# A graph network's gathers start ahead of the last chunk's table, with that chunk's share added from counts, and strip work moved into the layer's end

## What is computed

```python
h = relu(layernorm(x)); h = relu(h @ enc_w1.T + enc_b1) @ enc_w2.T + enc_b2
for w in conv_w:                                   # 5 layers
    m = h @ w
    agg = segment_sum(m[src], dst, num_segments=12500)
    gi, gh = agg @ gru_wih.T + gru_bih, h @ gru_whh.T + gru_bhh
    r, z = sigmoid(ir + hr), sigmoid(iz + hz)      # thirds of gi and gh
    n = tanh(i_n + r * h_n)
    h = (1 - z) * n + z * h
h = relu(h)
x + sigmoid(relu(h @ dec_w1.T + dec_b1) @ dec_w2.T + dec_b2)
```

## Time and profile before

| | |
|---|---|
| timed runs, median (lowest, highest) | 4899.29 us (4897.4, 4904.11) |
| profiled execution, span from the first to the last instruction | 4906.3 us |
| PE busy | 4601.4 us, 94% |
| ACT busy | 3823.5 us, 78% |
| POOL busy | 3459.9 us, 71% |
| DVE busy | 2117.3 us, 43% |
| DMA | 1215.98 MB, mean 248 GB/s |

### The profile page before, as it was taken

The page is one execution under the profiler, slowest core; times in us unless marked ns, Lnnn a source line. Parts: engine busy times, 40 slices in busy tenths (PEclk is TensorE's granted clock), DMA queues, the critical chain, the costliest instruction groups (busy, mean ns, idle before and its releaser), DMA issues.

```text
span 4906.3 us, 65249 instructions
## 1 busy us (share of the span) xinstructions
PE 4601.4 (94%) x21744; PEld 3523.0 (72%) x21744; DVE 2117.3 (43%) x5021; ACT 3823.5 (78%) x3047; POOL 3459.9 (71%) x3554
## 2 busy tenths in 40 slices
PE   5579999999799999989999999899999989999998
PEld 3357767776587777767777777677777767777775
DVE  7678878878423333332333333232323322333334
ACT  5479999998588888858888887788878758787785
POOL 3577667666477777767777777677777767767675
PEclk8789999999999999999999999999999989999999
DMA  6899999999877777787777779777777877777775
GB/s 210 282 287 278 282 279 289 271 279 293 280 231 240 241 234 245 233 297 243 234 239 241 236 241 310 225 239 235 247 229 248 289 235 225 221 214 220 217 219 154
DMA packets 711002, 1215.98 MB, mean 248 GB/s; under 512 B 282849, under 2 KB 441570, under 8 KB 710562
## 3 DMA queue, kind: packets, MB, share of 16 engines
q1 hardware_dynamic: 540992, 748.04, 49.5%
q0 software_dynamic: 169264, 462.12, 29.9%
q10 hardware_dynamic: 434, 1.81, 0.1%
HBM read 1015.23 MB, written 196.41 MB: 247 GB/s over the span
## 4 chain that ended last, share of the span: by engine, by line
PE 69%; ACT 9%; POOL 7%; issue 6%; DMA 5%; DVE 3%; SPq 1%; DVEq 0%; POOLq 0%; ACTq 0%
PE strip_ps L1908 33%; PE four_ps L1908 16%; POOL messages L940 7%; ACT counts L1126 6%; PE agg_ps L1801 3%; PE four_ps L1801 3%; DMA raw<-adjacency 3%; ACT room L1101 2%; PE r_ps L1817 2%; PE z_ps L1817 1%; PE r_ps L1823 1%; PE z_ps L1823 1%; PE four_ps L1824 1%; PE r_ps L1830 1%; PE four_ps L1894 1%
## 5 line engine op out<-in xcount | busy, mean ns | idle before, releaser
L940 POOL DMA_INDIRECT messages<-table,src_stage x3503 | 3412.8, 974 | 1355.4 <-issue 1088.3
L1126 ACT ACTIVATE counts<-raw 128x2048 fp32r<-128x2048 uint8 x1382 | 2277.8, 1694 | 408.7 <-PE strip_ps L1908 222.7
L1908 PE MATMUL strip_ps<-counts,parts 128*128 128x512 f32 x9212 | 2338.7, 407 | 65.6 <-ACT counts L1126 55.3
L1908 PEld LDWEIGHTS strip_ps<-counts,parts 128*128 128x128 f32 x9212 | 1724.3, 190 | 531.3 <-issue 122.6
L1908 PE MATMUL four_ps<-counts,parts 128*128 128x512 f32 x4116 | 985.4, 396 | 0.0
L1126 ACT ACTIVATE counts<-third_raw 128x2048 fp32r<-128x2048 uint8 (+1 forms) x522 | 856.3, 1689 | 158.7 <-PE strip_ps L1908 89.2
L1908 PEld LDWEIGHTS four_ps<-counts,parts 128*128 128x128 f32 x4116 | 768.8, 188 | 184.0 <-issue 28.3
L1410 DVE TENSOR_TENSOR selection<-agg_ps,dst_stage 128x1024 fp32r<-128x1024 bf16 (+1 forms) x269 | 327.7, 1218 | 943.0 <-PE agg_ps L1808 942.2
L1410 DVE TENSOR_TENSOR selection<-four_ps,dst_stage 128x1024 fp32r<-128x1024 bf16 (+1 forms) x172 | 207.9, 1209 | 864.7 <-PE four_ps L1808 864.6
L1101 ACT ACTIVATE room<-four_ps 128x784 uint16<-128x784 f32 x448 | 363.6, 826 | 86.7 <-PE four_ps L1894 54.6
L1801 PE MATMUL agg_ps<-messages,selection 128*128 128x256 f32 x2147 | 329.9, 297 | 37.7 <-DMA messages<-table,src_stage 37.7
(11 more groups left out here) (226 smaller groups left out, 3560.3 us busy)
## 6 DMA issues: line engine op xcount, KB each, us to landing
raw<-adjacency SPq DMA_DIRECT2D x691, 448.0 KB, 4.8
third_raw<-adjacency SPq DMA_DIRECT2D x261, 448.0 KB
adjacency<-room SPq DMA_DIRECT2D x112, 784.0 KB
parts<-table SPq DMA_DIRECT2D x35, 1792.0 KB, 13.9
messages<-table,src_stage POOLq DMA_INDIRECT x3503
table<-table_stage SPq DMA_DIRECT2D x108, 512.0 KB, 3.1
h_old<-states SPq DMA_DIRECT2D x120, 256.0 KB
states<-h_new SPq DMA_DIRECT2D x108, 256.0 KB, 3.5
```

The source lines that it names most:

```text
L940: nc.gpsimd.indirect_dma_start(messages[:, slot, t, :, :].rearrange("p i f -> p (i f)").bitcast(F32), None, table[k.layer % 2], bass.Indir ...
L1126: nc.scalar.activation(to, raw_piece[:, :, a * EIGHTH:e * EIGHTH].rearrange("p q (k d) -> p k q d", d=EIGHTH), ACT.Copy).then_inc(expanded, 1)
L1908: last = mm(strip_banks[k.bank_of(i)], parts[:, block, half, :], counts[:, 0 if k.first else p % 2, at, :], start=(p == 0 and at == 0 and ...
```

## The change

From layer 2 on, POOL may start when the tables of chunks 0 to 23 are stored. The first 3 groups of the layer (24 tiles) gather without the last chunk's rows: edges whose source is in chunk 24 have their source set to 0 and their destination moved out of the one-hot's reach. Their share, which touches at most 256 columns of sums, is added from a small matrix of counts (`late_counts`, 2 source blocks by 256 columns), built once in layer 1 by one-hots on DVE and products on PE, in the bank `dec_ps`, so that layer 1's strips have one bank only. At each layer's end (layers 1 to 3) `move` for chunk 23 comes one step earlier, its last phases are drawn together in the last step, the gates' work goes ahead of the last three groups on PE and DVE, and the following layer's 8 pieces are dealt out between the last chunk's phases. Slots turn by layer so that the first group of a layer goes into the slot that is free first.

```diff
+EARLY = 3
+EARLY_TILES = EARLY * GT
+FIRST_LATE = 2
+FOLLOWING_PE, FOLLOWING_ACT = (1, 1, 0), (1, 1, 1)
...
+        self.early = EARLY if layer > 1 else 0
+        self.passes_on = 0 < layer < LAYERS - 1
+        self.tail = self.steps - TAIL_GROUPS + 1 if self.passes_on else self.steps
...
+    def phase_at(self, chunk, t):
+        if self.passes_on and chunk == LAST - 1 and t > 3:
+            return self.steps - 1 if t <= 5 else self.gru_at[chunk] + t - 2
+        return self.gru_at[chunk] + t - 1
...
+    def slot_of(self, s):
+        return (s + self.layer) % SLOTS
     def bank_of(self, i):
-        return i % 2 if 0 < self.layer < LAYERS - 1 else 0
+        return i % 2 if 1 < self.layer < LAYERS - 1 else 0
...
# POOL
-                pool.wait_ge(table_stored, 16 * CHUNKS * (k.layer + 1))
-                gather_half(k, k.c0 - 1, 1, [STEPS - 1])
-                both_halves(k, k.c0)
+                if k.early:
+                    pool.wait_ge(table_stored, 16 * (CHUNKS * (k.layer + 1) - 1))
+                    gather_half(k, k.c0 - 1, 1, [STEPS - 1], LAST * CHUNK)
+                    gather_half(k, k.c0, 0, range(k.early - 1), LAST * CHUNK)
+                    pool.wait_ge(table_stored, 16 * CHUNKS * (k.layer + 1))
+                    gather_half(k, k.c0, 0, range(k.early - 1, SLOTS))
+                    gather_half(k, k.c0, 1, range(SLOTS, STEPS))
...
# SP, after the steps
+                    for u, pieces in enumerate(k.following_pieces(FOLLOWING_ACT)):
+                        states_and_tables(k.steps + u)
+                        if u == 4:
+                            next_portion(k, PORTIONS - 1)
+                            load_old(0, J, 0, following.v - 1)
+                            load_fold(layer + 1)
+                        if u != 3:
+                            for i, p in pieces:
+                                load_after(DENSE_CHUNKS + i, p)
+                        if u == 4:
+                            for i, p in k.following_pieces(FOLLOWING_ACT)[3]:
+                                load_after(DENSE_CHUNKS + i, p)
...
# ACT, after the steps
+                    for u, pieces in enumerate(k.following_pieces(FOLLOWING_ACT)):
+                        if u < len(FOLLOWING_ACT):
+                            for i, p in pieces:
+                                expand(following, i, p)
+                            gru_steps(k.steps + u)
+                        else:
+                            gru_steps(k.steps + u)
+                            for i, p in pieces:
+                                expand(following, i, p)
...
# DVE
+            def late_one_hots(tile):
+                wait(dve, late_built, tile)
+                ops.tensor_scalar(late_low, late_cols, late_sources[:, tile:tile + 1], None, ALU.is_equal)
+                ops.tensor_scalar(late_dst, late_cols, late_nodes[:, tile:tile + 1], None, ALU.is_equal).then_inc(late_hot, 1)
...
                 for step in range(k.steps):
+                    at_once = step >= k.tail - 1 or step == k.steps - 1
                     select_next(k, c, s, TAIL_GROUPS)
+                    if step < k.tail:
+                        add_previous(k, c, s, sum_used)
+                    if k.early and step == k.late_add_at():
+                        add_late(k, c, s)
+                    if step >= k.tail:
+                        gru_steps(step)
                     combine(k, c, s)
+                    if at_once:
                         add(k, c, s)
+                    if k.passes_on and step == k.tail - 1:
+                        move(k, c, sum_used)
+                    if step < k.tail:
+                        gru_steps(step)
                     if step in strip_ends:
                         strip_done(strip_ends[step])
+                    if layer == 1 and FIRST_LATE <= step < FIRST_LATE + EARLY_TILES:
+                        late_one_hots(step - FIRST_LATE)
...
# PE
+                def build_late(tile):
+                    pe.wait_ge(late_hot, tile + 1)
+                    for block in range(LATE_BLOCKS):
+                        last = mm(dec_ps[:, block * LATE_COLS:(block + 1) * LATE_COLS], late_low[:, block * P:(block + 1) * P], late_dst, ...)
+                    last.then_inc(late_built, 1)
+                def sum_late():
+                    pe.wait_ge(late_ready, 1)
+                    pe.wait_ge(table_out, k.v + CHUNKS)
+                    for block in range(LATE_BLOCKS):
+                        for half in range(2):
+                            last = mm(table_ps[:, 0:LATE_COLS], parts[:, LAST * J + block, half, :], late_counts[:, block, :], ...)
...
                 for step in range(k.steps):
+                    if step >= k.tail:
+                        gru_steps(step)
                     sum_group(k, c, s)
...
+                    if step < k.tail:
+                        gru_steps(step)
                     sum_pieces(k.pieces_at(step))
+                    if k.early and step == k.strip_end(0):
+                        sum_late()
                     if step < k.steps - 1:
                         place_group(k, c, s)
+                    if layer == 1 and FIRST_LATE <= step < FIRST_LATE + EARLY_TILES:
+                        build_late(step - FIRST_LATE)
...
+                    for u, pieces in enumerate(k.following_pieces(FOLLOWING_PE)):
+                        gru_steps(k.steps + u)
+                        for i, p in pieces:
+                            sum_piece(following, i, p)
```

More of the change, by code:

```diff
@@ L194, in __init__ @@
         self.old = [sum(e.old_loads[i] for e in earlier) for i in range(2)]
-        self.tiles_before = [sum(tiles_of(c, s) for e in earlier for c, s in e.groups if s % SLOTS == slot) for slot in range(SLOTS)]
+        self.tiles_before = [sum(tiles_of(c, s) for e in earlier for c, s in e.groups if e.slot_of(s) == slot) for slot in range(SLOTS)]
         self.spread_gru()
@@ L245, in active @@
     def active(self, step):
-        return [(chunk, step - self.gru_at[chunk] + 1) for chunk in self.order if 1 <= step - self.gru_at[chunk] + 1 <= G_LAST]
+        return [(chunk, t) for chunk in self.order for t in range(1, G_LAST + 1) if self.phase_at(chunk, t) == step]
+    def phase_at(self, chunk, t):
+        if self.passes_on and chunk == LAST - 1 and t > 3:
+            return self.steps - 1 if t <= 5 else self.gru_at[chunk] + t - 2
+        return self.gru_at[chunk] + t - 1
     def gathered(self, c, s):
@@ L848, in layers @@
                     next_portions(k, step)
-                if not last_layer:
-                    load_fold(layer + 1)
+                if last_layer:
+                    for step in range(k.steps, k.steps + G_LAST):
+                        states_and_tables(step)
+                else:
[11 more added lines that the diff above has]
+                                load_after(DENSE_CHUNKS + i, p)
             def general():
@@ L940, in gather_half @@
                         nc.gpsimd.indirect_dma_start(
-                            messages[:, slot, t, :, :].rearrange("p i f -> p (i f)").bitcast(F32), None, table[k.layer % 2],
+                            messages[:, slot, t, :, :].rearrange("p i f -> p (i f)").bitcast(F32), None, table[k.layer % 2][0:until, :],
                             bass.IndirectOffsetOnAxis(ap=src_stage[:, at:at + 1], axis=0)).then_inc(gathered[slot], 16)
@@ L1482, in before_candidate, with add_late @@
+            def add_late(k, c, s):
+                dve.wait_ge(agg_added, c * STEPS + (k.group + s))
+                dve.wait_ge(carried, k.c0 + k.carry0)
+                dve.wait_ge(late_summed, k.layer - 1)
+                ops.tensor_tensor(running[:, 0:LATE_COLS], running[:, 0:LATE_COLS], table_ps[:, 0:LATE_COLS], ALU.add).then_inc(late_added, 1)
+                dve.wait_ge(late_added, k.layer - 1)
             def before_candidate(v, j):
@@ L1631, in layers @@
                 strip_ends = {k.strip_end(i): i for i in range(DENSE_CHUNKS)}
-                stage_src(c0 - 1, 1)
-                stage_src(c0, 0)
+                if not k.early:
+                    stage_src(c0 - 1, 1)
+                    stage_src(c0, 0)
                 if layer == 1:
@@ L1789, in sum_group @@
                 g = c * STEPS + (k.group + s)
[L1790 removed]
+                slot = k.slot_of(s)
                 n_tiles = tiles_of(c, s)
@@ L2020, in last_chunk_step @@
                         decode_second(n, LAST_J)
+                def build_late(tile):
+                    pe.wait_ge(late_hot, tile + 1)
+                    for block in range(LATE_BLOCKS):
+                        last = mm(dec_ps[:, block * LATE_COLS:(block + 1) * LATE_COLS], late_low[:, block * P:(block + 1) * P], late_dst,
+                                  start=(tile == 0 and block == 0), stop=(tile == EARLY_TILES - 1 and block == LATE_BLOCKS - 1), skip_group_check=True)
+                    last.then_inc(late_built, 1)
[4 more added lines that the diff above has]
```

(6 more changed lines are left out.)

114 lines of the change are left out of this document (86 added, 28 removed).

## The result

The change made nothing faster; the kernel is 0.2% slower. On one chip, in turn, the kernel before took 4904.23 us (median of 12 runs, 4897.40 to 4908.12) and the changed one 4914.51 us (12 runs, 4907.91 to 4922.91): ratio 1.0023 [1.0014, 1.0031]. The forecast was 4873.3. One execution among the experiments, 5384.33 us at a lower granted clock (0.813), is left out.

The account below looks back on a forecast made before the run. POOL's gathers and one pause were taken to bound layers 1 to 3, PE layer 4. Gains of 1.8 + 12.6 + 12.0 - 0.5 = 25.9 us gave 4873.3 us, range 4859 to 4888 for 8 in 10.

Parts of the forecast that it names:

- What bounds the kernel: Layers 1 to 3 are as long as POOL's gathers (860 us) plus one pause (22.8); in layer 4 PE bounds.
- What PE needs for chunk 23: At a layer's end, PE's path from group 80's transposes to chunk 23's store at 2190.6 has 5.2 us to spare.
- my 7.1: Chunk 23's table is issued for store by SP 7.1 us after the layer's last gather.
- A landing of 3.1: At a layer's end, chunk 23's table takes 3.1 us from SP's issue to POOL's start, giving a 10.2 us pause.
- Third end: I take 43.7: Into layer 4, PE reaches its first group 43.7 us after POOL's last gather instead of 55.7, gaining 12.0 us.
- Layer 4 as long as before from there: From PE's first group of layer 4 on, the layer takes as long as before the change.
- Layer 1's extra: PE's added work and waits in layer 1 from one strip bank, count products and one-hots: 16 us, within 15.0 to 18.9.
- the first end: End of layer 1: the shorter pause would bring 12.6 us, but layer 1's added PE time leaves a 1.8 us gain.
- DVE's one-hots hold POOL: Rival: in layer 1, 48 one-hots each block a gather, 19 us in all, total gain 17.7, 4882 us; chance 0.04.
- PE becomes the bound in layers 2 and 3: Rival: PE gets no slack in these layers, each gives back some 4 us; gain 18, 4881 us; chance 0.12.
- The sum: 1.8 + 12.6 + 12.0 for the three layer ends, less 0.5 for sum_late in layer 4: 25.9 us gained.
- That rival's 4914 us: Rival: in layer 1 each tile's products wait for one-hots, 2 us a tile, 57 us, giving 4914 us; chance 0.04.

Follow-up runs that it names:

- e7_noearly: e3_both without early gathering: POOL waits for the whole table, no counts are built, layer 1 has two strip banks; 4899.43 us, ratio 1.0000.
- e3_both: e1_order's edit on the changed kernel, plus SP's late portion ahead of chunk 23's store and two raw loads ahead of the last portion; 4876.72 us, 0.9945.
- e1_order: Changed kernel with one reorder: in step 80 DVE does chunk 13's update ahead of group 80's add and move; 4891.85 us, ratio 0.9974.
- e10_raw: e1_order plus, on SP, the raw loads of pieces 10 and 11 ahead of the last portion of parts; 4875.40 us, ratio 0.9948.
- e8_phase: e4_both2 with chunk 23's phases 3 to 5 a step earlier, ahead of group 82's sum, and portion 3 behind chunk 13's table; 4871.89 us, 0.9943.
- e4_both2: e3_both with 2 early groups in place of 3, so 16 tiles of counts instead of 24; 4875.82 us, ratio 0.9937.

## Why the prediction was wrong

**What bounds the kernel**: right for the kernel before, where the early gather is what opens the gain (e7_noearly has none). It no longer holds after the change. In e3_both layers 2 and 3 take 869.0 and 871.0 us, which is the forecast's 871, but partly by luck: the pauses are 13.1 and 15.4 us and not 10.2, and the rest comes from the gathers between them, 855.9 and 855.6 us where they took 861.0 before. (Some 2 of these 5 us are one gap of POOL 16 us into the layer, 2.53 us in layer 2 before, which the later traces do not have; why was not tested.)

**"What PE needs for chunk 23"**: the step that failed. This path was given 15.0 us from group 80's transposes (2175.6) to the store (2190.6) and 5.2 us to spare. I computed this path from group 80's transposes with `add` and `move` "behind chunk 13's transposes and the first products", and gates "from 2176.4 on", right after the transposes. The diff says the reverse on DVE: `at_once` puts `add` and `move` ahead of `gru_steps`, chunk 13's update among them, and PE's order puts chunk 13's transposes ahead of chunk 23's gates. PE waits for DVE, which waited for PE: 4.0 us, then up to 3.1 more at half clock, and the path takes 20.6 to 21.8 us. In e1_order it takes 15.0 to 15.4, as computed. I read the new place of the moved call and not what it was now ahead of. With the order mended the store comes at +8.9 to +10.3 us in e1_order and e3_both, still 2 to 3 over my 7.1. That rest is the other half of the step: the spare time. The path is as long as computed, but it starts late. Before, PE has group 80's rows transposed 13.1 to 14.4 us before the last gather ends, in the changed kernel 6.3, in e3_both 5.4 to 5.6. Where it starts earlier, at 9.4 and 9.3 us in layers 2 and 3 of e10_raw, the store comes at +6.2 and +6.7 and the pauses are 10.64 and 11.16.

**"A landing of 3.1"**: mis-sized. I took it from chunk 24's store of 256 KB; chunk 23's 512 KB take 3.8 at best from issue to POOL's start, and 4.4 to 6.2 with a portion right behind. Nor do chunk 24's 256 KB always take 3.1: in e7_noearly they take 4.8 to 6.3, and why was not tested.

**"Third end: I take 43.7"**: the mechanism was named (the raw load behind the last portion) and mis-sized. Piece 10's load was issued at 3989.70, 36.2 us after the last gather, where I had it right behind a portion 24 us after. Ten of these 12 us are the portion itself, at 34.1: chunk 24's transposes come 27.5 us after the last gather where I had 19.4, behind chunk 23's delay (in e1_order chunk 24's table goes at 22.6 to 23.3, not 29.6). The other 2 are `h_old` and the folded weights, which stand between portion and raw load in SP's queue. The wait is 7.97, and the first group comes at 56.6, a loss of 0.8 where 12.0 was to be gained. With DVE's order mended the first group comes at 51.3 (e1_order), and with the raw loads ahead too at 37.6 (e10_raw): the queue's order is worth most of this.

**"Layer 4 as long as before from there"**: nearly so in the changed kernel (896.1 us after 894.5), wrong as a rule; where PE comes earlier the wait for raw bytes moves behind its first group and takes 4.8 us back (e3_both).

**Layer 1's extra**: right within 2 us (18.0 for 16; bank 6.2 and 6.3), and POOL 8.7 us late for 7.1. It ate the first end as forecast, and with the fault on top turned it into a loss of 4.7.

**DVE's one-hots hold POOL** (rival): not seen. In the groups by line of the changed kernel the gathers of layer 1 take the 968 ns of before, beside the 48 one-hots:

```profile
L1000 POOL DMA_INDIRECT messages<-table,src_stage x665 | 643.6, 968 | 212.9 <-issue 197.5 <-PE agg_ps L1941 11.1 <-PE four_ps L1941 4.3
```

The Trainium skill's page "SBUF — State Buffer", section "Who interferes with whom", has a DVE instruction in a 2-port perf mode and GpSimd block each other for the whole instruction. The profile does not name the mode of these 48, which take 292 and 307 ns each; had each held a gather for its length, the 665 gathers would be some 14 us longer in all, 0.02 us each, and none of that shows.

**PE becomes the bound in layers 2 and 3** (rival, chance 0.12): this came true at the layers' ends, in the changed kernel already. The chain of work that ended last, by engine, before and after:

```profile
PE 69%; ACT 9%; POOL 7%; issue 6%; DMA 5%; DVE 3%; SPq 1%; DVEq 0%; POOLq 0%; ACTq 0%
PE 78%; ACT 9%; DMA 5%; issue 3%; DVE 3%; POOL 1%; SPq 0%; DVEq 0%; ACTq 0%; POOLq 0%
```

POOL's gathers, which before are the chain up to each layer's end, are all but gone from it (1 to 2% in e1_order, e3_both and e10_raw too). PE's waits from the end of layer 1's gathers to the end of layer 2's say the same, first before (2189 to 3073 us), then after (2194 to 3074 us):

```profile
PE four_ps L1801 <- DMA messages<-table,src_stage: 7.0, 2, 4.7
PE strip_ps L1908 <- ACT counts L1126: 6.0, 2, 3.6
...
PE agg_ps L1801 <- DMA messages<-table,src_stage: 1.8, 1, 1.8
```

```profile
PE strip_ps L2048 <- ACT counts L1194: 9.3, 1, 9.3
PE four_ps L1883 <- DVE h_new L1644: 6.7, 2, 4.0
```

The 8.8 us of waits for messages are gone; what is left are the two faults and the update of chunk 23. POOL in turn waits for a slot for up to 2.3 us at a time in layers 2 and 3 (0.3 before), the sign that the prediction named. So what PE loses at a layer's end or start now lengthens the layer, and the raw loads count in every layer. It is also what ends the road at 870 us (e8_phase).

**The sum**: forecast 25.9 us. The traces give, first gather to first gather, -4.7, +2.6, +2.0 and -3.4: -3.5. In the medians 10.3 us are lost where 25.9 were to be gained, 36 short. DVE's order accounts for 22.7 of them (4914.51 to 4891.85, on two chips) and SP's for 15.1 (4891.85 to 4876.72). With both mended the kernel gains 29.6 us on its chip (e3_both) or 25.2 (e10_raw): the sum was that of a kernel without the two faults, with its total right and its terms not, since the pauses gained less and the gathers more. My chance of 0.04 for slower rested on layer 1's extra alone; I priced no mishap of order on DVE or SP. That rival's 4914 us is the measured time by chance only: it had 57 us of extra in layer 1, and there are 18.0.

**Open**: executions of one kernel scatter over some 15 us here (4907.9 to 4922.9), and no trace of a typical run of the changed kernel was taken. The best versions, e4_both2, e8_phase, e10_raw and e3_both, lie at 0.9937 to 0.9948, and the intervals do not tell them apart.

## What to carry to other kernels

When a call moves in an in-order engine's list, write down for each engine what it is now ahead of, and follow that to the engine that it waits for: two engines that each put the other's wait first cost more than the step that was moved. A transfer on the critical path needs its whole queue looked at, since every load between it and its trigger is paid for, and one swap of issues (raw bytes ahead of a portion) was here worth 15 to 19 us, where the main idea with DVE's order mended had gained 14.5 (4906.35 to 4891.85). A pause that is taken away must be followed by the question who needed it: here 10 to 17 of POOL's 23 us stayed in every version with DVE's order mended, with PE late at most layers' ends.

## What the runs showed of the hardware

- A wait of 4.00 us on PE was followed by a stretch at half granted clock (0.50), of some 3.5, 5 and 6 us at the three ends, in which a pair of 128x512 products took 1.91 us instead of 1.02; the same products after no wait ran at 1.00 (e1_order). The wait cost 5.9 to 7.1 us in all.
- A store of 512 KB held its reader for 3.8 to 4.1 us at 16 of 21 ends at which the last portion before it was issued 7 to 11 us ahead, and for 4.3 to 5.7 at the other five. With a load of 1.8 MB issued 0.5 us behind it, it was 4.4 to 4.6 us at eight of nine ends and 6.2 at one.
- Gathers were not slowed by 16-bit one-hots on DVE: 968 ns each with 48 of them in the layer and without.
